# Second feed-forward product from three bfloat16 pieces of the weighted Gelu outputs, in half batches

## The reference, cut to what matters

```python
def quantize_w8_per(w, axis):
    amax = jnp.clip(jnp.max(jnp.abs(w), axis=axis, keepdims=True), 1e-08, None)
    scale = 127.0 / amax
    w_q = jnp.clip(jnp.round(w * scale), -128.0, 127.0) / scale
def quantize_a16(x):
    amax = jnp.clip(jnp.max(jnp.abs(x)), 1e-08, None)
    scale = 32767.0 / amax
    x_q = jnp.clip(jnp.round(x * scale), -32768.0, 32767.0) / scale
W_in_sim = quantize_w8_per(W_in, axis=0)
W_out_sim = quantize_w8_per(W_out, axis=1)
hidden = jax.nn.gelu(x_sim @ W_in_sim + b_in, approximate=False)
out = quantize_a16(hidden) @ W_out_sim + b_out        # added to x
```

## Time and profile before

| | |
|---|---|
| time, median of 3 runs (range) | 3090.8 us (3089.63 to 3092.59) |
| span of the profiled execution | 3157.6 us, 57839 instructions |
| mean granted clock of TensorE over the span | 0.951 |
| busy: PE / weight load / DVE / ACT / POOL | 87% / 66% / 65% / 52% / 23% |
| the down stage in the profile | from 2918.8 us to the end |
| matmuls of the down stage (L2319) | 1024, 223.2 us busy, 381 ns mean |

### The profile page before, as it was taken

The page is one execution under the profiler, slowest core; times in us unless marked ns, Lnnn a source line. Parts: engine busy times, 40 slices in busy tenths (PEclk is TensorE's granted clock), DMA queues, the critical chain, the costliest instruction groups (busy, mean ns, idle before and its releaser), DMA issues. The chain is left out here.

```text
span 3157.6 us, 57839 instructions
## 1 busy us (share of the span) xinstructions
PE 2733.3 (87%) x20742; PEld 2084.7 (66%) x20743; DVE 2058.2 (65%) x3869; ACT 1649.1 (52%) x2861; POOL 714.3 (23%) x690
## 2 busy tenths in 40 slices
PE   8999889996776899999689999688888888476899
PEld 6777644454665788888677787555555555365788
DVE  5666648886233232111389999689999999676544
ACT  3333357775222222222256666499999999588000
POOL 0111104444455000000333321122222220200600
PEclk9999889998887899999899999799999999799999
DMA  3000252223555444444411110000110000144554
GB/s 127 1 1 1 77 189 84 83 82 121 200 174 186 150 140 143 143 145 137 140 42 41 39 37 20 22 23 28 28 29 28 28 28 21 42 198 188 195 190 146
DMA packets 131042, 291.61 MB, mean 92 GB/s; under 512 B 21008, under 2 KB 57872, under 8 KB 122128
## 3 DMA queue, kind: packets, MB, share of 16 engines
q1 hardware_dynamic: 104336, 228.99, 21.2%
q0 software_dynamic: 17792, 51.40, 4.9%
q10 hardware_dynamic: 8704, 8.39, 0.8%
HBM read 184.90 MB, written 103.81 MB: 91 GB/s over the span
## 5 line engine op out<-in xcount | busy, mean ns | idle before, releaser
L1293 ACT ACTIVATE cx_h<-bank,c_b 128x256 f32<-128x256 f32 (+1 forms) x288 | 117.6, 459 | 387.7 <-PE bank L1245 387.7
L1952 DVE TENSOR_SCALAR e_low<-bank 128x2048 f32<-128x2048 f32 x128 | 293.3, 2292 | 30.2 <-PE bank L1845 30.2
L1245 PE MATMUL bank<-cx_zT,cx_w 128*128 128x256 f32 (+1 forms) x1152 | 249.6, 370 | 2.0 <-DMA cx_w<-cw_dram 1.1
L1827 ACT ACTIVATE e_low<-e_low 128x2048 f32<-128x2048 f32 x128 | 244.7, 1912 | 4.1
L1256 PE MATMUL bank<-c_w,cx_h 128*128 x1088 | 246.6, 379 | 0.0
L1825 ACT ACTIVATE e_low<-e_low 128x2048 f32<-128x2048 f32 x128 | 243.6, 1903 | 0.0
L2319 PE MATMUL bank<-wout,fd_q 128*128 128x256 f32 x1024 | 223.2, 381 | 20.6 <-DVE fd_q L2338 20.6
L1245 PEld LDWEIGHTS bank<-cx_zT,cx_w 128*128 128x128 f32 x1152 | 211.6, 192 | 30.0 <-DMA cx_w<-cw_dram 1.5
L2319 PEld LDWEIGHTS bank<-wout,fd_q 128*128 128x128 f32 x1024 | 195.9, 191 | 47.8 <-DVE fd_q L2338 20.9
L1256 PEld LDWEIGHTS bank<-c_w,cx_h 128*128 128x128 f32 x1088 | 201.2, 190 | 24.4
L1845 PE MATMUL bank<-e_qT,e_kT 32*128 32x256 f32 x2048 | 148.8, 404 | 67.9 <-DVE e_high L1953 67.1
(11 more groups left out here) (375 smaller groups left out, 6402.5 us busy)
## 6 DMA issues: line engine op xcount, KB each, us to landing
cx_w<-cw_dram SPq DMA_DIRECT2D x72, 512.0 KB, 3.3
hidden<-fu_h SPq DMA_DIRECT2D x32, 1024.0 KB, 3.9
fd_h<-hidden SPq DMA_DIRECT2D x32, 1024.0 KB, 5.1
cx_rows<-expert_rows SPq DMA_DIRECT2D x64, 256.0 KB, 3.2
slot_y<-cx_y POOLq DMA_DIRECT2D x64, 256.0 KB, 2.6
g_cT<-ctxT_dram SPq DMA_DIRECT2D x32, 256.0 KB, 5.0
queries<-g_qT SPq DMA_DIRECT2D x32, 256.0 KB, 5.8
b_qT<-queries SPq DMA_DIRECT2D x32, 256.0 KB
```

The lines of the kernel that those rows point to most:

```text
L1245: last = nc.tensor.matmul(H[k][f // 2][:, (f % 2) * GROUP_ROWS:(f % 2) * GROUP_ROWS + cols], w1[k][:, c, f * P:(f + 1) * P], zT[k][:, c, 0 ...
L1827: nc.scalar.activation(flat(low[n % RING][:]), flat(low[n % RING][:]), ACT.Exp, scale=-1.0).then_inc(low_ready, 1)
L1952: nc.vector.tensor_scalar(flat(low[n % RING][:]), HEADS4.rearrange("p r s -> p (r s)"), -1.0, 0.0, ALU.mult, ALU.max).then_inc(neg_ready, 1)
```

## The change

Each batch is cut in two halves of 4 of the 8 feature groups, so that there are 64 units, with four buffers each. The step of the weights' rows moves to the activations: `wout` keeps whole numbers up to 127, which bfloat16 holds exactly, and each rounded Gelu output is multiplied by its row's step. That product is a float32 number, which is split into three bfloat16 pieces: the upper 16 bits of the float32 word (read in place, with a step of two bfloat16 elements), the upper 16 bits of what remains (`rest`), and the last remainder (`low`).

In a unit, ACT scales and rounds the 4 groups (`counted`, 1024 columns, in place), takes the offset off two of them (`whole`, 512 columns) and weighs those two (`weighed`, twice 256 columns). DVE weighs the other two (twice 256 columns), takes the first piece off all four (`remains`, 1024 columns) and makes the last piece of one (`lowest`, 256 columns); GpSimd makes the last piece of the other three (768 columns). PE makes 24 bfloat16 products of 128x128 by 128x256 in the place of 8 float32 ones. DVE adds a batch to `X` after every second unit. The loads wait only for their buffers, the stores move from ACT's to SP's queue behind the loads, four batches late, and the bias is added on GpSimd in `ffn_up`. Loops with a counter give way to instructions written out. In `run_experts` the last scaling of `wout` is dropped, and the weights are loaded to a tile of that stage.

```diff
@@ -872,7 +872,7 @@
         s = {"prob": t["prob"], "slot": t["slot"], "y": t["slot_y"],
...
-             "wi": sb("wi", [P, FC, D]),
+             "wi": sb("wi", [P, FC, D]), "wo": sb("wo", [P, FC, D]),
...
@@ -928,7 +928,7 @@
...
-            for dst, src in ((s["w2"], "cw2"), (s["b1"], "cb1"), (s["b2"], "cb2"), (s["wi"], "fwi"), (t["wout"], "fwo")):
+            for dst, src in ((s["w2"], "cw2"), (s["b1"], "cb1"), (s["b2"], "cb2"), (s["wi"], "fwi"), (s["wo"], "fwo")):
...
@@ -1316,8 +1316,8 @@
...
-            ch = Chain(dve, weight_steps, 14)
-            w = (s["wi"], t["wout"])
+            ch = Chain(dve, weight_steps, 13)
+            w = (s["wi"], s["wo"])
...
@@ -1371,8 +1371,6 @@
                     scaled(0, inv)
                 elif i == 4:
                     scaled(1, inv)
-                else:
-                    scaled(1, t["amax"])
...
@@ -2159,7 +2157,15 @@
...
+        bo_added = sem("bo")
         block = ctx.enter_context(nc.Block())
+        @block.gpsimd
+        def _(pool):
+            with pool.Fori(0, B) as b:
+                x = t["X"][:, bass.ds(b * TB, TB), :]
+                nc.gpsimd.tensor_tensor(x, x, s["bo"][:, None, :].to_broadcast([P, TB, D]), ALU.add).then_inc(bo_added, 1)
+            pool.wait_ge(bo_added, B)
         @block.sync
         def _(sp):
@@ -2271,87 +2277,156 @@
     with ctx:
         sem = signals(nc, ctx, "fd_")
         sb = lambda n, shape, dt=FP: ctx.enter_context(nc.sbuf_tensor("fd_" + n, shape, dt))
-        LANES = range(PAIR)
-        h = [sb(f"h{p}", [P, FC, S]) for p in LANES]
-        q = [sb(f"q{p}", [P, FC, S]) for p in LANES]
+        HALVES, RING = 2, 4
+        HALF = FC // HALVES
+        UNITS, BY_ACT, BY_POOL = B * HALVES, 2, 3
+        h = [sb(f"h{k}", [P, HALF, S]) for k in range(RING)]
+        q = [sb(f"q{k}", [P, BY_ACT, S]) for k in range(2)]
+        top_part = [sb(f"p{k}", [P, HALF, S]) for k in range(RING)]
+        rest = [sb(f"rest{k}", [P, HALF, S]) for k in range(RING)]
+        low = [sb(f"low{k}", [P, HALF, S], BF) for k in range(RING)]
         top, topall = sb("top", [P, 1]), sb("topall", [P, 1])
-        steps, all_ready, root, q0, q_ready, o_raw, x_done, bo_added, took_pool_wait = (
-            sem(n) for n in ("steps", "all", "root", "q0", "q", "o_raw", "x_done", "bo", "took_pool_wait"))
-        h_in = [sem(f"h_in{p}") for p in LANES]
+        (steps, all_ready, root, scale_ready, t_ready, q_ready, by_act, by_dve, rest_ready, low_by_pool, low_by_dve, o_raw, x_done) = (
+            sem(n) for n in ("steps", "all", "root", "scale", "t", "q", "by_act", "by_dve", "rest", "low_by_pool", "low_by_dve", "o_raw", "x_done"))
+        h_in = [sem(f"h_in{k}") for k in range(RING)]
         x_out = sem("x_out")
         rows_out = out.rearrange("(n p) d -> p n d", p=P)
-        O = lambda p: bank[p]
+        sh, ish = s["scale"][:, 2:3], s["scale"][:, 3:4]
+        upper = lambda a: a.bitcast(BF)
+        factor = lambda half, f: t["amax"][:, 1, half * HALF + f:half * HALF + f + 1]
+        O = lambda b: t["psum"][:, 2 * (b % 2):2 * (b % 2) + 2, 0:D]
         block = ctx.enter_context(nc.Block())
         @block.sync
         def _(sp):
-            with sp.Fori(0, TRIPS) as i:
...
+            def store(b):
+                tiles = slice(b * TB, (b + 1) * TB)
+                sp.wait_ge(x_done, b + 1)
+                sp.dma_start(rows_out[:, tiles, :], t["X"][:, tiles, :]).then_inc(x_out, 16)
+            for n in range(UNITS):
+                b, half = n // HALVES, n % HALVES
+                own = slice(half * HALF, (half + 1) * HALF)
+                if n >= RING:
+                    sp.wait_ge(by_act, n - RING + 1)
+                    sp.wait_ge(by_dve, n - RING + 1)
+                sp.dma_start(h[n % RING][:], hidden[b][:, own, :]).then_inc(h_in[n % RING], 16)
+                if half and b >= 4:
+                    store(b - 4)
+            for b in range(B - 4, B):
+                store(b)
+            sp.wait_ge(x_out, 16 * B)
         @block.gpsimd
         def _(pool):
             nc.gpsimd.partition_all_reduce(topall[:], s["top"][:], P, ALL_MAX).then_inc(all_ready, 1)
-            with pool.Fori(0, B) as b:
-                x = t["X"][:, bass.ds(b * TB, TB), :]
-                nc.gpsimd.tensor_tensor(x, x, s["bo"][:, None, :].to_broadcast([P, TB, D]), ALU.add).then_inc(bo_added, 1)
+            for n in range(UNITS):
+                pool.wait_ge(rest_ready, n + 1)
+                if n >= RING:
+                    pool.wait_ge(o_raw, n - RING + 1)
+                r = rest[n % RING]
+                nc.gpsimd.tensor_tensor(low[n % RING][:, 0:BY_POOL, :], r[:, 0:BY_POOL, :], upper(r[:])[:, 0:BY_POOL, 1:2 * S:2], ALU.subtract).then_inc(low_by_pool, 1)
         @block.scalar
         def _(act):
             act.wait_ge(all_ready, 1)
             nc.scalar.activation(top[:], topall[:], ACT.Sqrt).then_inc(root, 1)
-            for b in range(B):
...
+            act.wait_ge(scale_ready, 1)
+            def counted(n):
+                act.wait_ge(h_in[n % RING], 16 * (n // RING + 1))
+                nc.scalar.activation(h[n % RING][:], h[n % RING][:], ACT.Identity, scale=sh, bias=MAGIC).then_inc(t_ready, 1)
+            def whole(n):
+                act.wait_ge(t_ready, n + 1)
+                if n > 1:
+                    act.wait_ge(by_act, n - 1)
+                nc.scalar.activation(q[n % 2][:], h[n % RING][:, 0:BY_ACT, :], ACT.Identity, bias=-MAGIC).then_inc(q_ready, 1)
+            def weighed(n):
+                act.wait_ge(q_ready, n + 1)
+                if n >= RING:
+                    act.wait_ge(o_raw, n - RING + 1)
+                for f in range(BY_ACT):
+                    last = nc.scalar.activation(top_part[n % RING][:, f, :], q[n % 2][:, f, :], ACT.Copy, scale=factor(n % HALVES, f))
+                last.then_inc(by_act, 1)
+            counted(0)
+            for n in range(UNITS):
+                if n + 1 < UNITS:
+                    counted(n + 1)
+                whole(n)
+                weighed(n)
         @block.tensor
         def _(pe):
-            nc.tensor.sem_inc(o_raw, PAIR)
...
+            def products(n, piece, pick):
+                b, half = n // HALVES, n % HALVES
+                for m in range(TB):
+                    for f in range(HALF):
+                        last = nc.tensor.matmul(O(b)[:, m, :], pick(n, f, m), s["wout"][:, half * HALF + f, :],
+                                                start=half + piece + f == 0, stop=half == HALVES - 1 and piece == 2 and f == HALF - 1)
+                return last
+            first = lambda n, f, m: upper(top_part[n % RING][:])[:, f, 2 * m * P + 1:2 * (m + 1) * P:2]
+            second = lambda n, f, m: upper(rest[n % RING][:])[:, f, 2 * m * P + 1:2 * (m + 1) * P:2]
+            third = lambda n, f, m: low[n % RING][:, f, m * P:(m + 1) * P]
+            for n in range(UNITS):
+                if n % HALVES == 0 and n >= 2 * HALVES:
+                    pe.wait_ge(x_done, n // HALVES - 1)
+                pe.wait_ge(by_act, n + 1)
+                pe.wait_ge(by_dve, n + 1)
+                products(n, 0, first)
+                pe.wait_ge(rest_ready, n + 1)
+                products(n, 1, second)
+                pe.wait_ge(low_by_pool, n + 1)
+                pe.wait_ge(low_by_dve, n + 1)
+                products(n, 2, third).then_inc(o_raw, 1)
         @block.vector
         def _(dve):
             dve.wait_ge(root, 1)
             ch = Chain(dve, steps, 4)
-            sh, ish = s["scale"][:, 2:3], s["scale"][:, 3:4]
             quantiser(nc, ch, top, sh, ish)
...
-            nc.vector.sem_inc(q0, PAIR)
...
+            nc.vector.sem_inc(scale_ready, 1)
+            def weighed(n):
+                dve.wait_ge(t_ready, n + 1)
+                if n >= RING:
+                    dve.wait_ge(o_raw, n - RING + 1)
+                for f in range(BY_ACT, HALF):
+                    last = nc.vector.tensor_scalar(top_part[n % RING][:, f, :], h[n % RING][:, f, :], MAGIC, factor(n % HALVES, f), ALU.subtract, ALU.mult)
+                last.then_inc(by_dve, 1)
+            def remains(n):
+                dve.wait_ge(by_act, n + 1)
+                dve.wait_ge(by_dve, n + 1)
+                p = top_part[n % RING]
+                nc.vector.tensor_tensor(rest[n % RING][:], p[:], upper(p[:])[:, :, 1:2 * S:2], ALU.subtract).then_inc(rest_ready, 1)
+            def lowest(n):
+                dve.wait_ge(rest_ready, n + 1)
+                r = rest[n % RING]
+                nc.vector.tensor_tensor(low[n % RING][:, BY_POOL:HALF, :], r[:, BY_POOL:HALF, :], upper(r[:])[:, BY_POOL:HALF, 1:2 * S:2], ALU.subtract).then_inc(low_by_dve, 1)
+            def add(b):
+                x = t["X"][:, b * TB:(b + 1) * TB, :]
+                dve.wait_ge(o_raw, HALVES * (b + 1))
+                nc.vector.scalar_tensor_tensor(x, O(b), ish, x, ALU.mult, ALU.add).then_inc(x_done, 1)
+            weighed(0)
+            for n in range(UNITS):
```

(37 more changed lines are left out.)

## The result

The changed kernel takes 3105.9 us in the median (3101.2 to 3109.2, 4 runs) against 3091.1 (3089.6 to 3092.6) for the kernel before: 14.7 us or 0.5% slower, ratio 1.005, 95% interval 1.0037 to 1.0062. Forecast were 3120, +29.

What follows compares the result with a forecast made beforehand. PE bound the down stage before; DVE, pushed by GpSimd, was to bound it at 3.7 us a unit. Down stage 12.9 plus up stage 16 gave 29 us on 3090.8: 3120 us, range 3045 to 3150.

Steps and rivals of the forecast that it cites:

- Direction and bound: Whole kernel 29 us slower (chance of slower 0.66); in the down stage DVE the bound instead of PE.
- PE's unit: Down stage: 24 bfloat16 matmuls a unit at 0.109 us each, 2.62 us a unit, 168 us in all.
- rival 2: Down stage: strided weight loads at float32's pace, 4.36 us a unit, PE the bound; total 3164 us; chance 0.06.
- the lower end: Down stage: a strided weight load costs what the packed one does, hidden behind the matmul's 0.109 us.
- GpSimd's push: Down stage: GpSimd's 768 columns, 1.7 us less 0.3 overlap, push DVE's work except the addition by 1.4 us.
- DVE's own work: Down stage, each unit: weighings 0.6, `remains` 1.22, `lowest` 0.43, addition 0.37 us; with gaps 2.65 us.
- Head: Opening of the down stage: all-reduce some 5.7 us late, step known at 2925.8, first `remains` at 2929.8.
- Bias in the up stage: Up stage: 32 GpSimd additions slow DVE's batch to 8.7 instead of 5.4 us; 16 us lost, from 0 to 22.
- At no cost: Dropped scaling in the experts' stage, loads and stores (178 GB/s), and PE's 1.1 us pauses add no time.
- The first rival: Down stage: exclusion doesn't bind long two-input DVE instructions; unit is ACT's 2.8 us; total 3049 us; chance 0.25.
- the third: Down stage: exclusion holds but GpSimd takes 1.3 us, 3.3 a unit; total 3087 to 3095 us; chance 0.07.
- the signs that I had named: Down stage: weighing or `lowest` 1.5 to 1.8 us in turn, GpSimd 1.6 to 1.9 unheld, DVE near 100% busy.

Runs made afterwards that it cites:

- experiments 1: Changed kernel, GpSimd's last pieces still made but waited for only by buffer reuse, PE reading zeros instead: 3103.2 us, down stage 234.9.
- experiment 2: Changed kernel with GpSimd's last-piece instruction left out, PE reading zeros instead (result incomplete): 3052.2 us, down stage 187.2.
- experiment 3: Changed kernel without the output bias (no 32 GpSimd additions in the up stage): 3080.9 us, ratio 0.997 to the kernel before.
- 5: Changed kernel with GpSimd making the last piece of one group instead of three, DVE of three: ratio 0.9973 to the kernel before.
- 6: Changed kernel with GpSimd making the last pieces of two groups instead of three, DVE of two: ratio 1.0003 to the kernel before.
- 7: Kernel before, with only the 32 GpSimd bias additions moved to the up stage: ratio 1.006 to the kernel before.
- experiment 4: Changed kernel with one more GpSimd all-reduce right behind the bias additions in the up stage: 3098.8 us, ratio 1.0024 to the kernel before.
- experiment 8: Changed kernel with 32 GpSimd memsets in place of the bias additions: 3158.8 us, on a chip where the kernel before took 3165.7.

## Why the prediction was right

**Direction and bound: right, but the direction rests on the bias alone.** DVE fills the down stage, GpSimd's instructions push it, PE waits (experiments 1 and 2 show it; the profile's 189 of 190 us had said so). Of the forecast +29 us, 12.9 were to come from the down stage, which came out 2.5 us shorter instead. The measured +14.7 is half of the forecast, and without the bias term the change would have been a small gain (experiment 3: 0.3% less than before). What I had only assumed, that DVE's long two-input instruction and GpSimd exclude each other, held: in the up stage the largest square went from 2.29 to 3.13 us in the mean and single bias additions up to 3.34, and in the last units of the down stage a `remains` issued behind a GpSimd instruction took twice its 1.21 us:

```profile
3093.42 1.71 POOL L2329 TENSOR_TENSOR fd_low<-fd_rest 128x768 bf16<-128x768 f32 x1 [2.02 <-DVE fd_rest L2408]
...
3093.71 2.49 DVE L2408 TENSOR_TENSOR fd_rest<-fd_p 128x1024 f32<-128x1024 f32 x1
```

**PE's unit, 2.62 us: right** (experiment 2). The strided weight loads (rival 2; `fd_p` and `fd_rest`) take what the packed ones (`fd_low`) do, 98 ns in the median of 512 (min/median/max):

```profile
L2368 PEld LDWEIGHTS bank<-wout,fd_p x512: 97/98/151, 2880.6 to 3096.7; 128*128 128x128 bf16 x171
...
L2368 PEld LDWEIGHTS bank<-wout,fd_rest x512: 97/98/151, 2882.1 to 3097.6; 128*128 128x128 bf16 x171
...
L2368 PEld LDWEIGHTS bank<-wout,fd_low x512: 95/98/99, 2885.7 to 3098.8; 128*128 128x128 bf16 x171
```

So the lower end, which the prediction took, holds.

**GpSimd's push, 1.4 in even and 0.71 beyond the addition in odd units: about right in the sum.** Measured 1.22 (1.82-0.60) and 0.81 (1.24-0.43), on average 1.01 where I had 1.05. GpSimd's instruction alone is 1.47 us, below my lower bound of 1.56, since I scaled its fixed part too: 256, 512 and 768 columns take 0.61, 1.04 and 1.47 us, which is 0.43 for 256 columns and 0.18 besides. In part this is luck: 0.18 us too much in even units and 0.10 too little in odd ones cancel, so the sum is closer than its terms.

**DVE's own work: the term that was mis-sized.** I had 2.65 us a unit, from mean durations; it is 3.41-1.01 = 2.40. A DVE instruction that doesn't need the result of the one ahead starts before that one has ended by the profile: the addition starts 1.14 us after a `remains` of 1.21 us, `lowest` 0.66 after an addition of 0.74, the weighing 0.34 after a `lowest` of 0.43. Where `lowest` follows the `remains` that it reads, it starts 1.24 us after it. I had taken the overlap from busy time over count for the weighing alone. The unit is 3.41 instead of 3.7, and 63x0.29 = 18 us came off the forecast.

**Head: too small.** The all-reduce came 8.8 us late, not 5.7, and the first `counted` began 10.1 us after the opening (2876.93-2866.83), where the forecast had 7.0 (2925.8-2918.8). In experiments 1, 2, 5 and 6, where loads run at that time as well, it was 7.3 to 7.4, in 7, where none do, 5.7; so 8.8 is more than this stage mostly shows. That loads in flight slow it is an argument from these numbers and was not tried by itself. The forecast +12.9 for the down stage with -18 and +3 is -2, and -2.5 was measured.

**Bias in the up stage, 16 us: right,** 14.8 measured, 14.4 and 15.3 by its removal and by itself. All five DVE lines grew in the stretch in which GpSimd worked. GpSimd's additions came 1.83 us apart (56.68 over 31); five to a batch of 8.7 us, as forecast, would be 1.74. The lines of before that they are measured against, and then those of after, which answer to the earlier trace rows too:

```profile
L2247 DVE TENSOR_SCALAR fu_zhi<-fu_z x32: 427/427/428, 2732.4 to 2898.7; 128x512 bf16<-128x512 f32 x32
...
L2249 DVE SCALAR_TENSOR_TENSOR fu_zlo<-fu_z,fu_zhi x32: 691/691/693, 2732.9 to 2899.1; 128x512 bf16<-128x512 f32 x32
...
L2260 DVE TENSOR_TENSOR f_top<-f_top,fu_one x32: 158/158/160, 2748.5 to 2916.3; 128x1 f32<-128x1 f32 x32
```

```profile
L2263 DVE CUSTOM_DVE_ANT_0 fu_square<-fu_h 128x2048 f32<-128x2048 f32 x7 | 21.9, 3129 | 1.8 <-ACT fu_h L2196 1.5 <-DVE f_top L2266 0.4
L2255 DVE SCALAR_TENSOR_TENSOR fu_zlo<-fu_z,fu_zhi 128x512 bf16<-128x512 f32 x7 | 11.4, 1634 | 0.2
L2253 DVE TENSOR_SCALAR fu_zhi<-fu_z 128x512 bf16<-128x512 f32 x7 | 9.6, 1370 | 0.2
L2251 DVE TENSOR_SCALAR fu_z<-f_z,f_scale 128x512 f32 x7 | 7.4, 1062 | 3.9 <-PE bank L2219 3.9
L2266 DVE TENSOR_TENSOR f_top<-f_top,fu_one 128x1 f32<-128x1 f32 x6 | 6.6, 1098 | 0.2
```

```profile
2673.83 56.68 POOL L2167 TENSOR_TENSOR X<-X,f_bo 128x512 f32 x31 [0.31 <-issue]
```

0.43 became 1.37 (L2253), 0.69 became 1.63 (L2255), 0.16 became 1.10 (L2266), 2.29 became 3.13 (L2263). The bias itself began 7.35 us after the stage opened (2672.26 against 2664.91), behind the all-reduce of `ffn_rows`.

**At no cost: right** for loads, stores and clock, as experiment 2's full PE shows. The first rival (44 us less) needed GpSimd and DVE to run beside each other, and they don't; the third (a quicker GpSimd) comes nearest in the down stage, but mostly for another reason: DVE's own work is shorter. Of the signs that I had named, `lowest` at 1.24 us lies below the 1.5 to 1.8 stated, and GpSimd's 1.47 below 1.6.

## What to carry to other kernels

An engine that the profile shows idle is not free if its instructions and a busy engine's exclude each other. Before you give elementwise work to GpSimd, count the DVE instructions beside it that have two tensor inputs in SBUF or are of the kind of the weighing and the two roundings here (one tensor input, and pushed all the same), and charge each meeting with GpSimd's duration less 0.25 us. Tune a split between the two by its count of groups, and put GpSimd's work beside a DVE instruction that reads PSUM, as the addition here. For DVE's own load take the distances from start to start, not the durations.

## What the runs showed of the hardware that was not expected

- The change of GpSimd from `tensor_tensor` or `tensor_scalar` to the all-reduce costs 5.7 to 8.8 us at the next all-reduce, and an early all-reduce of anything takes it off the path (5.4 us of the down stage in experiment 4, 7 us of the time). From a memset to the all-reduce nothing was lost (experiment 8).
- The routing stage with its indirect transfers ran at 262 GB/s on one chip and at 167 to 181 on another, which is 64 us between the two profiles shown and 75 to 81 us in the times of the kernel before; this hides a change of 15 us in a comparison of two single profiles.
